# Queries projected straight into turned form in the cross attentions of layers 2 and 3 of a four-layer decoder

## The chip, the cores and the metric

One core of one Trainium2 chip runs the whole decoder in one launch. The metric is the device time of one execution in microseconds (us). The kernel before has a median of 3866.13 us over 3 runs (3862.26 to 3866.85).

## The reference, cut to what matters

The decoder has four layers, each an attention over the image context and a feed-forward part, both gated and added to x. The change touches the attentions of layers 2 and 3. For x as 4096 rows (64 batches of 64 tokens) of 256 numbers, with 16 heads of 16, they compute

```python
y = layernorm(x)
q = rms_norm(y @ Wq + bq) * gq
k = rms_norm(ctx @ Wk + bk) * gk
v = ctx @ Wv + bv
s = einsum('bqhd,bkhd->bhqk', q, k) / sqrt(16)
o = einsum('bhqk,bkhd->bqhd', softmax(s), v)
x = x + tanh(gate) * (o @ Wo + bo)
```

where `rms_norm(q)` divides a row of 256 by `sqrt(mean(q*q) + 1e-6)`. Each batch attends to its own 64 context rows. The root is one number per query row, and gq one number per column of q, so both can stand elsewhere in the product of q and k.

## The kernel before

The rows lie as 32 tiles of 128 rows (two batches) in `core.xs`. The phases of the decoder follow one another; the two that the change touches are `phase_cross` (called as `cr2` and `cr3`, once for each layer) and `KeysValues`, which makes the keys and values of both layers much earlier, beside `phase_scatter` of layer 0.

`phase_cross` is a software pipeline over the 32 tiles, written out by hand: each engine has a loop over the step s, and handles in it different tiles that lie up to seven steps apart. The engines meet at semaphores alone, and each engine works strictly in its written order. One step of the tensor engine (L1700 to L1716) has eight parts: `scores(s+1)`, `turn_y(s+4)`, `turn_probs(s)`, `project(s+3)`, `values(s-1)`, `turn_q(s+2)`, `turn_out(s-2)`, `project_out(s-3)`. A tile passes through them like this:

- VectorE takes mean and variance (L1773, L1785), GpSimd the root of the variance (L1588, L1590), VectorE writes y (L1809); PE turns y (L1614), ScalarE copies it out of PSUM (L1726).
- `project` (L1627) multiplies the turned y by Wq: 128 rows of queries by 256 columns, in PSUM. VectorE adds the bias (L1803).
- ScalarE squares the queries with a running sum per row (L1743, two instructions), GpSimd makes the root (L1594, L1596), VectorE multiplies the queries by root and by gq (`normalise`, L1765), PE turns them (`turn_q`, L1637), ScalarE copies them out of PSUM as `qT` (L1750).
- `scores` (L1650) multiplies qT by the keys, which lie in DRAM as blocks (`kbd`) and are loaded a tile at a time. VectorE takes the largest of each row and head (L1791) and subtracts it (L1795), ScalarE takes the exponential with the fixed scale 1/4 (L1737), PE turns the result (L1663), ScalarE copies it (L1733, twice a tile), `values` (L1677) multiplies it by the values, VectorE divides by the sum (L1814, L1818), PE turns (L1687), ScalarE copies (L1756), `project_out` (L1697) multiplies by Wo, and VectorE adds the gated result to x (L1778). GpSimd has added the gated bias to x before (L1602).

A product of f32 operands shows as two PE passes, each with a weight load of its own; a turn of an f32 tile of 128 by 128 as one.

`scores` waits for the copy of `qT` of its own tile, which ScalarE makes behind the exponential and the square of other tiles in the same step. `normalise` waits for the root, which waits for the square, which waits for the exponential.

`KeysValues` loads two weights, two biases and the key gain of each layer on SyncE's queue (`sync_start`), ten loads in all; PE's first product waits for all ten. Behind them on the same queue stand the context tiles and the expert weights of layer 0. It multiplies the keys by root and gain (`norm`, L1464) with the gain in `self.gain`.

## Time and profile before

| | |
|---|---|
| median of 3 runs | 3866.13 us |
| the profiled execution: time | 3858.92 us |
| its span | 3857.2 us |
| mean granted clock of TensorE | 0.865 |
| busy PE, VectorE, ScalarE, GpSimd | 2872.7, 2279.2, 1494.0, 882.5 us |
| layer 2 attention, first to last VectorE instruction | 2175.3 to 2380.9 us |
| layer 3 attention, the same | 2796.9 to 3002.4 us |

Times in rows are us from the start of the span. An engine's busy time is the time in which it has an instruction under way; matmuls overlap, so the start times of the next part say more than busy time. The two attentions take some 411 us of the span together.

### The profile page before, as it was taken

The page shows a single profiled execution, that of the slowest core. Times are in us where ns is not written, and L with a number is a line of the kernel's source. Part 1 is how long each engine was busy: PE and PEld are TensorE (multiplying, and loading weights), DVE is VectorE, ACT ScalarE, POOL GpSimd, SP SyncE. Part 2 cuts the span into 40 slices and gives each one's busy share as a digit, 9 for nine tenths or more (in the row PEclk, how much of TensorE's full clock was granted, in tenths as well). Part 3 has the DMA queues.
Part 4 walks back from the last instruction along what each step waited for, and adds up shares of the span by engine and source line. Part 5 has one row for each costly group of instructions (what it writes and reads, how often), then busy time and mean ns, then how long its engine had stood idle before and what let it go on. Part 6 is the DMA issues. An engine that isn't in the chain of part 4 may idle for free. (4 is left out here: it accounts for less than half of the span.)

```text
span 3857.2 us, 60679 instructions
## 1 busy us (share of the span) xinstructions
PE 2872.7 (74%) x19894; PEld 1814.9 (47%) x19894; DVE 2279.2 (59%) x5157; ACT 1494.0 (39%) x3085; POOL 882.5 (23%) x1238
## 2 busy tenths in 40 slices
PE   5388884365999983499536698999889509999993
PEld 4133334122555552233213476544467507888783
DVE  7699975475777766433478697888688520000003
ACT  5277771253222226399424354222255101111110
POOL 3111110475233337111100132000033061111110
PEclk7599995798999995599758799999999559999997
DMA  7766630899222225577000251000043031211214
GB/s 256 175 114 122 121 77 0 299 369 349 73 80 82 78 64 202 103 131 113 23 2 0 88 165 60 1 1 1 18 143 119 0 123 42 63 58 50 77 32 131
DMA packets 261307, 386.18 MB, mean 100 GB/s; under 512 B 56321, under 2 KB 188654, under 8 KB 260768
## 3 DMA queue, kind: packets, MB, share of 16 engines
q1 hardware_dynamic: 234192, 312.76, 30.3%
q0 software_dynamic: 25152, 68.22, 5.1%
q8 instruction: 159, 2.61, 0.3%
q10 hardware_dynamic: 1680, 1.57, 0.2%
q14 instruction: 124, 1.02, 0.1%
HBM read 227.75 MB, written 160.24 MB: 101 GB/s over the span
## 5 line engine op out<-in xcount | busy, mean ns | idle before, releaser
L2771 POOL DMA_INDIRECT rows_out<-e_out,e_tr_dest x224 | 234.6, 1047 | 874.3 <-DVE e_out L3394 523.0
L1183 ACT ACTIVATE a_pt<-a_psS 128x512 f32<-128x512 f32 x512 | 277.6, 594 | 151.9 <-PE a_psS L1081 147.5
L3394 DVE COPY e_out<-e_psD 128x512 f32<-128x512 f32 x40 | 27.7, 692 | 492.8 <-PE e_psD L3362 492.6
L1205 DVE TENSOR_REDUCE a_mx_sb<-a_psM 128x4 f32<-128x1024 f32 x256 | 293.0, 1216 | 17.3 <-PE a_psM L1064 16.1
L3162 PE MATMUL e_psG<-e_wgu,e_yT 128*128 x576 | 275.6, 601 | 27.0 <-ACT e_yT L3190 24.4
L1095 PE MATMUL a_psV<-a_pt,a_vt 128*18 128x256 f32 x4096 | 291.1, 386 | 2.1 <-issue 1.7
L3362 PE MATMUL e_psD<-e_w,e_hT 128*128 128x256 f32 x1280 | 290.2, 386 | 0.0
L3351 PE MATMUL e_psH<-e_yT,e_w 128*128 128x256 f32 x1280 | 285.2, 381 | 1.6 <-issue 0.8
L3294 ACT ACTIVATE e_hT<-e_psH 128x512 f32<-128x512 f32 x160 | 95.5, 597 | 453.1 <-PE e_psH L3351 453.1
L3362 PEld LDWEIGHTS e_psD<-e_w,e_hT 128*128 128x128 f32 x1280 | 245.8, 195 | 33.3
L3351 PEld LDWEIGHTS e_psH<-e_yT,e_w 128*128 128x128 f32 x1280 | 244.6, 191 | 35.7 <-issue 2.1
L1190 ACT ACTIVATE a_pt<-a_psS 128x1024 f32<-128x1024 f32 x256 | 241.7, 1043 | 12.6 <-PE a_psS L1081 12.4
L1081 PE MATMUL a_psS<-a_qa,a_ka 50*128 50x256 bf16 (+1 forms) x2048 | 193.1, 278 | 59.9 <-DMA a_ka<-n_pieces 36.4
L2707 POOL DMA_INDIRECT rows_in<-sc_y,sc_i x192 | 191.4, 997 | 68.2 <-issue 57.1
L3196 ACT ACTIVATE e_th<-e_gcap 128x256 f32<-128x256 f32 x144 | 60.0, 417 | 333.7 <-DVE e_ucl L3230 333.7
L1404 PE MATMUL kv_psK<-e_bgu,e_bd 128*128 128x512 f32 x256 | 127.7, 647 | 57.3 <-DMA e_bd<-ctxT 57.3
L3227 DVE TENSOR_TENSOR e_gub<-e_psG,e_bgu 128x512 f32<-128x512 f32 x144 | 99.4, 690 | 109.5 <-PE e_psG L3162 103.4
L1064 PE MATMUL a_psM<-a_ka,a_qa 48*128 48x256 bf16 x1024 | 105.9, 288 | 73.9 <-DVE a_res L1220 30.9
L1081 PEld LDWEIGHTS a_psS<-a_qa,a_ka 50*128 50x128 bf16 (+1 forms) x2048 | 74.1, 95 | 177.6 <-issue 81.1
L3179 PE MATMUL e_psO<-e_wd,e_hT 128*128 x576 | 149.3, 382 | 2.4 <-ACT e_hT L3202 1.6
L3162 PEld LDWEIGHTS e_psG<-e_wgu,e_yT 128*128 128x128 f32 x576 | 99.2, 192 | 101.4 <-issue 101.3
L1095 PEld LDWEIGHTS a_psV<-a_pt,a_vt 128*18 128x18 f32 x4096 | 86.4, 97 | 109.9 <-issue 67.8
(384 smaller groups left out, 5938.3 us busy)
## 6 DMA issues: line engine op xcount, KB each, us to landing
kbd<-e_bgu SPq DMA_DIRECT2D x64, 512.0 KB, 4.0
cr_kbd<-kbd SPq DMA_DIRECT2D x64, 512.0 KB, 3.3
rows_in<-zeros POOLq DMA_DIRECT2D x36, 522.0 KB, 6.6
e_xin<-rows_in SPq DMA_DIRECT2D x144, 128.0 KB
vbd<-e_bd SPq DMA_DIRECT2D x64, 272.0 KB, 4.2
cr_vbd<-vbd SPq DMA_DIRECT2D x64, 272.0 KB, 2.7
cq_rows<-rows_out SPq DMA_DIRECT2D x32, 512.0 KB, 5.8
e_w<-in_L_ffn_w_dram SPq DMA_DIRECT2D x16, 1024.0 KB, 7.6
```

What stands on the lines that cost most here:

```text
L1081: ins = pe.matmul(psS[:, (first + b) % S_BANKS, k * DIM:(k + 1) * DIM], at_tile(ka, rows(b, KR), t, h, slice(k * P, (k + 1) * P)), at_tile ...
L1095: ins = pe.matmul(psV[32 * q:32 * q + 2 * V, b, :], vt[:, t % 4, 2 * k + b, g, q, :], pt[:, probs(t, 4 * g + q), b, k, :], start=(g == 0 a ...
L1183: act.activation(pt[:, probs(t, h), b, :, :], psS[:, unit(t, h, b) % S_BANKS, :].rearrange("p (k c) -> p k c", k=KC), ACT.Exp, scale=scale ...
L1190: act.activation(pt[:, probs(t, h), :, :, :], psS[:, first:first + 2, :].rearrange("p b (k c) -> p b k c", k=KC), ACT.Exp, scale=scale).th ...
L1205: dve.tensor_reduce(mx[:, t % 2, :, h, :], psM[:, k % 2, :, :].rearrange("p b (f c) -> p b f c", f=2), AX_X, ALU.max).then_inc(ring_read, 1)
L1404: ins = pe.matmul(self.psK[:, u, :], self.ct[:, i % 4, k, :], self.w[:, layer, k, :], start=(k == 0), stop=(k == KC - 1))
L2707: pool.indirect_dma_start(out=rows_in[:, :], out_offset=bass.IndirectOffsetOnAxis(ap=index[u][:, k:k + 1], axis=0), in_=y[:, u, :], in_off ...
L2771: pool.indirect_dma_start(out=self.rows_out[0:limit, :], out_offset=bass.IndirectOffsetOnAxis(ap=self.dest[:, t:t + 1], axis=0), in_=rows, ...
L3162: ins = pe.matmul(psG[:, u, :], yT[:, u, k, :], wgu[:, e, k, :], start=(k == 0), stop=(k == KC - 1))
L3179: ins = pe.matmul(psO[:, u, 0:D], hT[:, u, k, :], wd[:, e, k, :], start=(k == 0), stop=(k == KC - 1))
L3351: ins = pe.matmul(psH[:, b, (f % 2) * R:(f % 2 + 1) * R], w1s[:, m, k, f * P:(f + 1) * P], yT[:, u, :, k, :], start=(k == 0), stop=(k == K ...
L3362: ins = pe.matmul(psD[:, u, tt * D:(tt + 1) * D], hT[:, u, f, tt * P:(tt + 1) * P], w2s[:, m, f, :], start=(f == 0), stop=(f == FC - 1))
```

## The change

It makes the queries directly in turned form and lets the root act later.

- `project` swaps its operands: Wq becomes the stationary side, the turned y the moving one, so the product has the 256 query columns on partitions (two blocks of 128) and the rows along it. It is made of four products of 128 columns instead of two of 256.
- VectorE adds the bias, now one number per partition, and writes `qT` itself, in three buffers instead of two. `normalise`, `turn_q` and the copy L1750 are gone.
- ScalarE squares `qT` (without a running sum); PE adds over partitions with a column of ones (`sum_squares`, in the place of `turn_q`); ScalarE copies the 128 sums out of PSUM; GpSimd makes the root with 1/16 in it, one step later than before.
- `scores` waits for the bias addition instead of the copy. The exponential takes the root as its scale, one number per row, and waits for it.
- gq is multiplied into the key gain, once: `KeysValues` loads gq of both layers (two more loads on SyncE's queue, twelve to wait for) and VectorE multiplies 128x512 once before the loop.
- The start of `phase_cross` still has five loads before its first wait: bq comes as two loads of 128 numbers, one to a partition, and the broadcast loads of bq and gq fall away.

```diff
@@ -1323,6 +1323,8 @@
+        self.query_gain = flat[:, 3584:4096].rearrange("p (l o) -> p l o", l=2)
+        self.gained = core.sem(n + "_gn")
@@ -1342,11 +1344,12 @@
     def sync_start(self, sp):
-        for layer, (wk, wv, bk, bv, gk) in enumerate(self.weights):
+        for layer, (wk, wv, bk, bv, gk, gq) in enumerate(self.weights):
+            sp.dma_start(self.query_gain[:, layer, :], gq.rearrange("(a n) -> a n", a=1).broadcast_to([P, DIM])).then_inc(self.w_loaded, 16)
@@ -1413,7 +1416,7 @@
             ins.then_inc(self.turned, 1)
-        pe.wait_ge(self.w_loaded, 16 * 10)
+        pe.wait_ge(self.w_loaded, 16 * 12)
@@ -1446,8 +1449,10 @@
             ins.then_inc(self.values_laid, 1)
     def vector_setup(self, dve):
-        dve.wait_ge(self.w_loaded, 16 * 10)
+        dve.wait_ge(self.w_loaded, 16 * 12)
+        dve.tensor_tensor(self.gain, self.gain, self.query_gain, ALU.mult).then_inc(self.gained, 1)
+        dve.wait_ge(self.gained, 1)
     def bias(self, dve, i):
@@ -1511,8 +1516,8 @@
-    q_done, q_ready, q_squared, q_based, q_rooted, q_normed, q_turned, q_copied = (
-        core.sem(n + k) for k in ("qd", "qr", "qs", "qb", "qo", "qn", "qt", "qc"))
+    q_done, q_ready, q_squared, q_summed, sum_copied, q_based, q_rooted, ones_made = (
+        core.sem(n + k) for k in ("qd", "qr", "qs", "qu", "uc", "qb", "qo", "om"))
@@ -1523,7 +1528,9 @@
-        gains = sb(ctx, n + "gains", [P, 3, DIM], F32)
+        bias_out = sb(ctx, n + "bo", [P, DIM], F32)
+        bias_q = sb(ctx, n + "bq", [P, KC], F32)
+        ones = sb(ctx, n + "ones", [P, 1], F32)
@@ -1533,10 +1540,8 @@
-        q = sb(ctx, n + "q", [P, 2, DIM], F32)
-        junk = sb(ctx, n + "junk", [P, DIM], F32)
-        qn = sb(ctx, n + "qn", [P, 2, DIM], F32)
-        qT = sb(ctx, n + "qT", [P, 2, KC, P], F32)
+        sqT = sb(ctx, n + "sqT", [P, 2, KC, P], F32)
+        qT = sb(ctx, n + "qT", [P, 3, KC, P], F32)
@@ -1558,8 +1563,9 @@
             def _(sp):
-                for m, v in enumerate((bq, gq, bo)):
-                    sp.dma_start(gains[:, m, :], v.rearrange("(a n) -> a n", a=1).broadcast_to([P, DIM])).then_inc(w_loaded, 16)
+                for k in range(KC):
+                    sp.dma_start(bias_q[:, k:k + 1], bq[k * P:(k + 1) * P].rearrange("(p a) -> p a", a=1)).then_inc(w_loaded, 16)
+                sp.dma_start(bias_out[:, :], bo.rearrange("(a n) -> a n", a=1).broadcast_to([P, DIM])).then_inc(w_loaded, 16)
                 def load_values(t):
@@ -1581,6 +1587,7 @@
             def _(pool):
+                pool.memset(ones[:, :], 1.0).then_inc(ones_made, 1)
@@ -1588,10 +1595,10 @@
-                    t = s + 3
+                    t = s + 2
-                        pool.wait_ge(q_squared, t + 1)
-                        pool.tensor_scalar(base[:, t:t + 1], square[:, t:t + 1], 1.0 / DIM, 1e-6, ALU.mult, ALU.add).then_inc(q_based, 1)
+                        pool.wait_ge(sum_copied, t + 1)
+                        pool.tensor_scalar(base[:, t:t + 1], square[:, t:t + 1], CW / DIM, CW * 1e-6, ALU.mult, ALU.add).then_inc(q_based, 1)
@@ -1609,7 +1616,7 @@
-                        pe.wait_ge(q_copied, t - 2)
+                        pe.wait_ge(sum_copied, t - 2)
                     ins.then_inc(y_turned, 1)
@@ -1623,23 +1630,26 @@
-                    for k in range(KC):
-                        ins = pe.matmul(psQ[:, 0, :], yT[:, u, k, :], wqs[:, k, :], start=(k == 0), stop=(k == KC - 1))
+                    for c in range(KC):
+                        for k in range(KC):
+                            ins = pe.matmul(psQ[:, 0, c * P:(c + 1) * P], wqs[:, k, c * P:(c + 1) * P], yT[:, u, k, :], start=(k == 0), stop=(k == KC - 1))
                     ins.then_inc(q_done, 1)
-                def turn_q(t):
+                def sum_squares(t):
-                    pe.wait_ge(q_normed, t + 1)
+                    if t == 0:
+                        pe.wait_ge(ones_made, 1)
+                    pe.wait_ge(q_squared, t + 1)
-                        pe.wait_ge(q_copied, t)
+                        pe.wait_ge(sum_copied, t)
-                        ins = pe.transpose(psT[:, 1, k * P:(k + 1) * P], qn[:, u, k * P:(k + 1) * P], core.ident[:, :])
-                    ins.then_inc(q_turned, 1)
+                        ins = pe.matmul(psT[:, 1, 0:1], sqT[:, u, k, :], ones[:, :], start=(k == 0), stop=(k == KC - 1))
+                    ins.then_inc(q_summed, 1)
                 def scores(t):
-                    u, m = t % 2, t % NK
-                    pe.wait_ge(q_copied, t + 1)
+                    u, m = t % 3, t % NK
+                    pe.wait_ge(q_ready, t + 1)
@@ -1709,7 +1719,7 @@
-                        turn_q(s + 2)
+                        sum_squares(s + 2)
@@ -1734,20 +1744,18 @@
-                        act.activation(prob[:, t % 2, :, :], prob[:, t % 2, :, :], ACT.Exp, scale=CW ** -0.5).then_inc(exped, 1)
+                        act.wait_ge(q_rooted, t + 1)
+                        act.activation(prob[:, t % 2, :, :], prob[:, t % 2, :, :], ACT.Exp, scale=rms[:, t:t + 1]).then_inc(exped, 1)
-                        if t:
-                            act.wait_ge(q_squared, t)
-                        act.activation(junk[:, :], q[:, t % 2, :], ACT.Square, accum_out=square[:, t:t + 1]).then_inc(q_squared, 1)
+                        if t >= 2:
+                            act.wait_ge(q_summed, t - 1)
+                        act.activation(sqT[:, t % 2, :, :], qT[:, t % 3, :, :], ACT.Square).then_inc(q_squared, 1)
-                        act.wait_ge(q_turned, t + 1)
-                        if t >= 2:
-                            for r in range(2):
-                                act.wait_ge(s_done[r], t - 1)
-                        act.activation(qT[:, t % 2, :, :], psT[:, 1, :].rearrange("p (k c) -> p k c", k=KC), ACT.Copy).then_inc(q_copied, 1)
+                        act.wait_ge(q_summed, t + 1)
+                        act.activation(square[:, t:t + 1], psT[:, 1, 0:1], ACT.Copy).then_inc(sum_copied, 1)
@@ -1757,16 +1765,8 @@
             def _(dve):
-                def normalise(t):
-                    u = t % 2
-                    dve.wait_ge(q_rooted, t + 1)
-                    if t >= 2:
-                        dve.wait_ge(q_turned, t - 1)
-                    dve.scalar_tensor_tensor(out=qn[:, u, :], in0=q[:, u, :], scalar=rms[:, t:t + 1], in1=gains[:, 1, :],
-                                             op0=ALU.mult, op1=ALU.mult).then_inc(q_normed, 1)
-                dve.tensor_scalar(gains[:, 2, :], gains[:, 2, :], gate, None, ALU.mult).then_inc(bias_scaled, 1)
+                dve.tensor_scalar(bias_out[:, :], bias_out[:, :], gate, None, ALU.mult).then_inc(bias_scaled, 1)
@@ -1777,8 +1777,6 @@
-                    if ok(s + 2):
-                        normalise(s + 2)
@@ -1797,10 +1795,12 @@
-                        if t >= 2:
-                            dve.wait_ge(q_squared, t - 1)
-                            dve.wait_ge(q_normed, t - 1)
-                        dve.tensor_tensor(q[:, t % 2, :], psQ[:, 0, :], gains[:, 0, :], ALU.add).then_inc(q_ready, 1)
+                        if t >= 3:
+                            for r in range(2):
+                                dve.wait_ge(s_done[r], t - 2)
+                            dve.wait_ge(q_squared, t - 2)
+                        dve.tensor_tensor(qT[:, t % 3, :, :], psQ[:, 0, :].rearrange("p (k c) -> p k c", k=KC),
+                                          bias_q[:, :].rearrange("p (k a) -> p k a", a=1).broadcast_to([P, KC, P]), ALU.add).then_inc(q_ready, 1)
@@ -3407,8 +3407,8 @@
-    key_weights = (tuple(a["L2_xattn_" + k] for k in ("Wk_img", "Wv_img", "bk_img", "bv_img", "gk_img")),
-                   (turned[1], turned[2], *(a["L3_xattn_" + k] for k in ("b_k_img", "b_v_img", "g_k_img"))))
+    key_weights = (tuple(a["L2_xattn_" + k] for k in ("Wk_img", "Wv_img", "bk_img", "bv_img", "gk_img", "gq")),
+                   (turned[1], turned[2], *(a["L3_xattn_" + k] for k in ("b_k_img", "b_v_img", "g_k_img", "g_q"))))
```

What stands on PE in one step of layer 2 before (cr_yT is the turned y, cr_wq the weight Wq, cr_psT and cr_psQ places in PSUM; here a product's two passes count as one):

```order
L1650 MATMUL cr_psS<-cr_kbd,cr_qT 64x256 x8
L1614 MATMUL cr_psT<-ident,cr_y 128x128 x2
L1663 MATMUL cr_psP<-ident,cr_prob 128x128 x8
L1627 MATMUL cr_psQ<-cr_wq,cr_yT 128x256 x2
L1677 MATMUL cr_psO<-cr_vbd,cr_pT 64x34 x16
L1637 MATMUL cr_psT<-ident,cr_qn 128x128 x2
L1687 MATMUL cr_psU<-ident,cr_o 128x128 x2
L1697 MATMUL cr_psQ<-cr_wo,cr_oT 128x256 x2
```

And now:

```order
L1660 MATMUL cr_psS<-cr_kbd,cr_qT 64x256 x8
L1621 MATMUL cr_psT<-ident,cr_y 128x128 x2
L1673 MATMUL cr_psP<-ident,cr_prob 128x128 x8
L1635 MATMUL cr_psQ<-cr_yT,cr_wq 128x128 x4
L1687 MATMUL cr_psO<-cr_vbd,cr_pT 64x34 x16
L1647 MATMUL cr_psT<-cr_ones,cr_sqT 128x1 x2
L1697 MATMUL cr_psU<-ident,cr_o 128x128 x2
L1707 MATMUL cr_psQ<-cr_wo,cr_oT 128x256 x2
```

The order of the eight parts is the same; the fourth has four products of half the width, and the sixth has two products of one column in place of two turns.

On VectorE, one step before, and one now:

```order
L1778 SCALAR_TENSOR_TENSOR xs<-cr_psQ,gates,xs 128x256
L1765 SCALAR_TENSOR_TENSOR cr_qn<-cr_q,cr_rms,cr_gains 128x256
L1785 BN_AGGR mv<-cr_st 128x2
L1791 TENSOR_REDUCE cr_mx_sb<-cr_psS 128x16
L1795 TENSOR_TENSOR cr_prob<-cr_psS,cr_mx_sb 128x1024
L1803 TENSOR_TENSOR cr_q<-cr_psQ,cr_gains 128x256
```

```order
L1778 SCALAR_TENSOR_TENSOR xs<-cr_psQ,gates,xs 128x256
L1783 BN_AGGR mv<-cr_st 128x2
L1789 TENSOR_REDUCE cr_mx_sb<-cr_psS 128x16
L1793 TENSOR_TENSOR cr_prob<-cr_psS,cr_mx_sb 128x1024
L1802 TENSOR_TENSOR cr_qT<-cr_psQ,cr_bq 128x256
```

The instruction between the addition to x and the reduction of the scores is gone; the others of the step stay in their order (beside those shown: L1809, L1814, L1818, L1773).

## Rows read from the trace of the kernel before

**Rows 1.** The page's busy time of each engine, share of the span, instructions.

```profile
PE 2872.7 (74%) x19894; PEld 1814.9 (47%) x19894; DVE 2279.2 (59%) x5157; ACT 1494.0 (39%) x3085; POOL 882.5 (23%) x1238
```

**Rows 2.** Windows: stretch, length, busy PE PEld DVE ACT POOL, clock, DMA share, GB/s.

```profile
2190.00:2200.00 10.00, 7.46 (x60) 5.77 (x61) 6.52 (x12) 5.55 (x13) 3.56 (x9) 0.83 0.33 105
2240.00:2280.00 40.00, 39.12 (x486) 29.69 (x485) 37.14 (x70) 24.22 (x56) 15.01 (x35) 1.00 0.46 143
```

**Rows 3.** Timeline, one step of layer 2, PE: start, length, instruction, [idle before <-releaser].

```profile
2261.77 1.09 PE L1650 MATMUL cr_psS<-cr_kbd,cr_qT 64*64 64x256 f32 x16
2262.79 0.44 PE L1614 MATMUL cr_psT<-ident,cr_y 128*128 128x128 f32 x2
2263.07 1.04 PE L1663 MATMUL cr_psP<-ident,cr_prob 128*128 128x128 f32 x8
2263.94 1.03 PE L1627 MATMUL cr_psQ<-cr_wq,cr_yT 128*128 128x256 f32 x4
2264.90 1.13 PE L1677 MATMUL cr_psO<-cr_vbd,cr_pT 128*64 128x34 f32 x32
2265.96 0.44 PE L1637 MATMUL cr_psT<-ident,cr_qn 128*128 128x128 f32 x2
2266.23 0.38 PE L1687 MATMUL cr_psU<-ident,cr_o 128*128 128x128 f32 x2
2266.45 1.03 PE L1697 MATMUL cr_psQ<-cr_wo,cr_oT 128*128 128x256 f32 x4
2267.61 0.64 PEld L1650 LDWEIGHTS cr_psS<-cr_kbd,cr_qT 64*64 64x64 f32 x16 [0.53 <-ACT cr_qT L1750]
```

**Rows 4.** Timeline, the same step, VectorE from `normalise` to the subtraction.

```profile
2262.39 0.94 DVE L1765 SCALAR_TENSOR_TENSOR cr_qn<-cr_q,cr_rms,cr_gains 128x256 f32<-128x256 f32 x1 [0.22 <-POOL cr_rms L1596]
2263.35 1.19 DVE L1791 TENSOR_REDUCE cr_mx_sb<-cr_psS 128x16 f32<-128x1024 f32 x1
2264.57 1.22 DVE L1795 TENSOR_TENSOR cr_prob<-cr_psS,cr_mx_sb 128x1024 f32<-128x1024 f32 x1
```

**Rows 5.** Timeline, weight loads of short products in layer 2's feed-forward part.

```profile
2444.41 0.19 PEld L2296 LDWEIGHTS bs_psC<-bs_mix,bs_scT 128*128 128x128 f32 x1 [0.24 <-issue]
2444.52 0.30 PEld L2303 LDWEIGHTS bs_psU<-bs_wu,bs_yT 128*128 128x128 f32 x2
...
2450.35 0.52 PEld L2257 LDWEIGHTS bs_psC<-bs_wr,bs_yT 128*128 128x128 f32 x4 [1.24 <-issue]
2450.79 0.30 PEld L2265 LDWEIGHTS bs_psG<-bs_wg,bs_yT 128*128 128x128 f32 x2
```

**Rows 6.** Waits, 2180 to 2590: total us, times, longest.

```profile
PEld cr_psS L1650 <- ACT cr_qT L1750: 23.5, 32, 3.2
```

**Rows 7.** Timeline, the pipeline of layer 2 filling: the first three tiles' scores.

```profile
2184.34 0.63 PE L1637 MATMUL cr_psT<-ident,cr_qn 128*128 128x128 f32 x2
...
2185.87 0.64 PEld L1650 LDWEIGHTS cr_psS<-cr_kbd,cr_qT 64*64 64x64 f32 x16 [1.30 <-ACT cr_qT L1750]
...
2191.43 0.64 PEld L1650 LDWEIGHTS cr_psS<-cr_kbd,cr_qT 64*64 64x64 f32 x16 [3.25 <-ACT cr_qT L1750]
...
2197.58 0.64 PEld L1650 LDWEIGHTS cr_psS<-cr_kbd,cr_qT 64*64 64x64 f32 x16 [1.35 <-ACT cr_qT L1750]
```

**Rows 8.** Timeline, the last steps of layer 2.

```profile
2355.09 0.64 PEld L1650 LDWEIGHTS cr_psS<-cr_kbd,cr_qT 64*64 64x64 f32 x16 [0.45 <-ACT cr_qT L1750]
...
2360.86 0.64 PEld L1650 LDWEIGHTS cr_psS<-cr_kbd,cr_qT 64*64 64x64 f32 x16 [0.68 <-ACT cr_qT L1750]
...
2364.45 1.03 PE L1697 MATMUL cr_psQ<-cr_wo,cr_oT 128*128 128x256 f32 x4
...
2366.23 0.64 PEld L1650 LDWEIGHTS cr_psS<-cr_kbd,cr_qT 64*64 64x64 f32 x16 [1.15 <-ACT cr_qT L1750]
```

**Rows 9.** The stage of the keys: a load on SyncE's queue, and a window (columns as in rows 2).

```profile
690.82 0.43 SPq L1349 DMA_DIRECT2D e_bgu<-in_L_xattn_g_k_img_dram  x1
...
740.00:780.00 40.00, 28.41 (x74) 12.08 (x73) 30.91 (x73) 20.45 (x72) 28.89 (x35) 0.94 0.97 353
```

More of the change, by code:

```diff
@@ L1498, in vector_end, with phase_cross @@
             self.lay(dve, i)
-def phase_cross(core, name, kbd_dram, vbd_dram, wq, bq, gq, wo, bo, gate, prefetch=None):
+def phase_cross(core, name, kbd_dram, vbd_dram, wq, bq, wo, bo, gate, prefetch=None):
     nc = core.nc
@@ L1601, in _ @@
                         pool.wait_ge(y_ready, t + 1)
-                        pool.tensor_tensor(core.xs[:, t, :], core.xs[:, t, :], gains[:, 2, :], ALU.add).then_inc(bias_added, 1)
+                        pool.tensor_tensor(core.xs[:, t, :], core.xs[:, t, :], bias_out[:, :], ALU.add).then_inc(bias_added, 1)
             @block.tensor
@@ L3475, in flamingo_decoder @@
         core.clear_semaphores()
-        phase_cross(core, "cr3", kbd[1], vbd[1], turned[0], a["L3_xattn_b_q"], a["L3_xattn_g_q"], turned[3], a["L3_xattn_b_o"], x_gate(3))
+        phase_cross(core, "cr3", kbd[1], vbd[1], turned[0], a["L3_xattn_b_q"], turned[3], a["L3_xattn_b_o"], x_gate(3))
         core.clear_semaphores()
```

2 lines of the change are left out of this document (1 added, 1 removed).

## The prediction, made before the changed kernel ran

> **What bounds the kernel now.** I read the page's shares first: PE is the busiest engine over the whole span [rows 1], but with 74% it does not bound every stage. So I went to windows in the two attentions. In the middle of layer 2's, PE is busy for 39.12 of 40 us and VectorE for 37.14, at full clock [rows 2]. Two engines near their end at once: only the timeline of one step tells which of them waits. The reader should see there that a step takes 5.84 us (scores of one tile at 2261.77, of the next at 2267.61) and that both engines are held up a little. PE's weight loads stand idle for 0.53 us before the scores, until ScalarE has copied qT [rows 3]; that wait comes with every tile, 23.5 us for the 32 of a layer [rows 6]. VectorE is idle for 0.22 us before `normalise`, until the root is there [rows 4]; its other nine instructions follow each other closely. The loop that sets the step runs through VectorE: subtraction, exponential, square, root, `normalise`, reduction, subtraction.
>
> **How much of PE's wait is real.** A change of tile shape costs PE something in any case. `project` (four passes of 256 columns) begins at 2263.94, and `values`, which nothing holds up, at 2264.90: 0.96 us. `project_out` has the same four passes and begins at 2266.45, so the scores could begin at 2267.41 and do so at 2267.61 [rows 3]. PE's own work in a step is thus 5.64 us, and 0.20 us is waiting. VectorE's own is 5.84 - 0.22 = 5.62. The two are nearly equal, and this decides the case: what leaves VectorE gives nothing below what PE then needs.
>
> **The change on VectorE.** `normalise` goes, 0.94 us [rows 4], and the wait before it: 5.84 - 0.22 - 0.94 = 4.68 us a step. The bias addition keeps its size (256 numbers a partition from PSUM, the added operand repeated as in the subtraction, whose 1024 numbers take 1.22 us beside the reduction's 1.19 [rows 4], so repetition costs nothing to speak of). VectorE no longer bounds.
>
> **The change on PE, step by step.**
> - `project`: eight passes of 128 columns instead of four of 256. Four such passes of the router have their weight loads from 2450.35 on, and the next product's load stands at 2450.79: 0.11 us a pass [rows 5]. The turns of the probabilities give 0.87 us for eight (2263.07 to 2263.94) [rows 3]. Eight passes take 0.87 to 0.90 us, four long ones 0.86; I take +0.03 us.
> - `sum_squares`: two products of one column, four passes, in place of two turns. No product of one column is in this trace. The nearest has 8 columns: its weight load at 2444.41 is followed by the next at 2444.52 [rows 5], so a pass takes 0.11 us although it has hardly any columns. Four passes 0.44 us, two turns 0.22 (2266.23 to 2266.45 [rows 3]): +0.22 us. From below: passes that hide wholly beside their neighbours leave only what the turns took, -0.22; from above 0.19 us a pass, the length of one load [rows 5], makes it +0.54. I take the spacing, since a load's length overlaps the pass ahead.
> - The wait before the scores goes: -0.20 us. `qT` is written by VectorE nearly two steps ahead.
>
> New PE step: 5.64 + 0.03 + 0.22 = 5.89 us, **0.05 more than now**. In the full steps the change gains nothing; the work moves to the engine that has none to spare.
>
> In the Trainium skill, TensorE: Matmul & The Clock Gate, Back-to-back issue gap, products of 1 to 64 columns follow at some 60 cycles, 25 ns. By that `sum_squares` would cost 0.1 us, the step would be 5.55 and the whole gain about 27 us, not 11. The Trainium skill has on the same page, in LDWEIGHTS (loading the stationary operand), a load of 128 columns take 128/1.2 = 107 ns; this trace's 0.11 us at 8 columns [rows 5] sides with the load.
>
> **What else waits.** After the scores are started, the chain scores 1.09, reduction 1.19, subtraction 1.22 and three hand-overs of 0.05 ends 3.7 us later, so the next scores never wait for `shifted` in a step of 5.89. `sum_squares` waits for ScalarE's square of a step before. ScalarE loses the accumulator read and the copy of 256 numbers and is busy for 24.22 of 40 us now [rows 2]; the exponential's root is made a step ahead. The prices of scale-by-row and of the 128x1 copy are not in the trace; from nothing to 0.2 us each, they lie under ScalarE's idle 40%. The new waits stand there too: behind the exponential's wait for the root on ScalarE are the square and the copy of the sums, and none of the three is late while the root is a step old. Should a VectorE instruction last longer in its new company, it has 1.2 us of new slack.
>
> **Filling.** Here the change does gain. In the first steps PE has few parts, and the loop through the root sets the pace: scores of tiles 0, 1 and 2 begin at 2185.87, 2191.43 and 2197.58 [rows 7], then every 5.84. Now:
> - tile 0: its scores wait for nothing behind `sum_squares(0)`, which begins where `turn_q(0)` did, at 2184.34, and takes four passes at the lower of the two clocks, twice 0.11 us each: it ends at 2185.2, the scores begin at 2185.3. Gain 0.6.
> - tile 0 to 1 and 1 to 2: bound by the chain of 3.7 us (PE's parts are 1.0 to 3.5). Gains 5.56 - 3.7 = 1.9 and 6.15 - 3.7 = 2.4.
> - tile 2 to 3: PE's parts without both output parts, 1.02 + 0.28 + 0.87 + 0.99 + 1.06 + 0.55 = 4.8. Gain 1.0. Tile 3 to 4: with `turn_out` 5.0. Gain 0.8.
>
> Together 6.7 us a layer. The granted clock averaged 0.83 in 2190 to 2200 [rows 2], so part of it was at 1.2 GHz, behind a wait of PE's loads of 3.25 us [rows 7]. The waits become shorter; if 3 us at 1.2 GHz stay and now fall on PE's own work, they take 1.5 us back.
>
> **Emptying.** The last step ahead of the final scores has neither `turn_y` nor `project`. In it PE could start those scores at 2364.45 + 0.96 + 0.22 = 2365.6 instead of 2366.23 [rows 8]: gain 0.6. The step before it, without `turn_y`, takes 5.77 (2355.09 to 2360.86 [rows 8]) and would take 5.89 - 0.28 + 0.06 = 5.67, if the change of shape costs a little more without the turn: gain 0.1. Behind the last scores nothing changes but the exponential's scale. Two steps ahead of these have a full load on PE and already less on VectorE, 5.77 too; there PE's 5.89 costs 0.12 each. Net gain 0.4.
>
> **Start of the phase.** Five loads stand ahead of the first wait, as before; two broadcasts of 128 KB are replaced by 256 pieces of 4 bytes. Nothing, +-0.5 us.
>
> **The keys' stage.** Two more loads on SyncE's queue, one every 0.47 us or so (the last of ten is issued at 690.82 [rows 9]): the context tiles and the expert weights behind them start 0.95 us later. The stage then is bound by transfers (DMA share 0.97 [rows 9]), so this stays: +0.95. The one VectorE product (128x512, like a bias addition) is done while PE makes its first products: 0.
>
> **The sum.** A layer: -6.7 (filling) + 23 x 0.05 = 1.15 (tiles 4 to 27) - 0.4 (emptying) = -5.95. Two layers -11.9, the keys' stage +0.95: **-11 us**. From the profiled execution's 3858.92 that is 3848; the median of the runs is 7.2 us higher than that execution, 3866.13, so I predict **3855** for the median.
>
> The Trainium skill, ScalarE: Activation LUTs, What ACT_TABLE_LOAD costs, adds about 93 ns to an ACTIVATE for a scale of one number per row. In the filling it would stand in the chain of some three exponentials a layer: the sum would be half a us less of a gain. No row here shows it.
>
> **The rivals.**
> 1. *The gain stays in the filling but half of it is lost* (clock low for a stretch, PE step 5.95 instead of 5.89). For it: PE's step was worked out from start times read to 0.01 us and from one change of shape of 0.96. Filling -13.4, clock +3, 46 x 0.11 = +5, emptying -0.8, keys +1: about -5, so 3861. Within 0.2%.
> 2. *PE's passes cost less than the load's spacing* (few columns are cheap after all, or the scores' change of shape costs less than the one before `values`). Between 5.45 (sums wholly hidden) and 5.89 I put the step at 5.6: 46 x 0.29 = 13 us more, 3842. Against it: spacings of 0.11 at 8 and at 128 columns alike [rows 5].
> 3. *Slower: PE's step grows by the loads' full length.* If the twelve short passes take 0.19 us each, the length of one load [rows 5], `project` is 1.52 and `sum_squares` 0.76 us: +0.65 and +0.32 a step. 46 x 0.97 = 45 us against the gain of 11: 3900. It decides from 6.3 us a step on, where 46 steps x 0.4 eat the gain and 8 us more. Against it: four such passes in a row took 0.44 [rows 5].
> 4. *The change does not free the scores*: they wait in the same place for the subtraction of the tile before. That chain is 3.7 us, so it would need 2 us of delays; it falls under rival 1.
>
> **How the numbers follow.** A measurement of this kernel tells about 0.2%, 7.7 us, from no change. The forecast has 0.56, rival 1 (with 4) 0.28, rival 2 0.07, rival 3 0.05, other losses of the slower kind 0.04. Most of the forecast's own width (3850 to 3859) is on the faster side of 3858.4; 0.04 of it and rival 1 are the middle. So faster 0.59, same 0.32, slower 0.09. The range takes in the forecast, rival 1 and the near part of rival 2: 3847 to 3866.
>
> **What would show it.** In the changed profile the step in the middle of layer 2 should be 5.85 to 5.93 us, with no wait on PE and VectorE idle for about 1.2 us; windows of 40 us should show VectorE at some 32 us. The scores should have no waits after tile 2, the weight loads of `sum_squares` should be 0.11 us apart, and the first two spacings of the scores 3.7 us. Each attention should be 6 us shorter, the keys' stage 1 us longer. A step under 5.75 or over 6.0 makes the prediction wrong, and so does a filling that gains less than 4 us.

## The result and the profile after

| | before | changed |
|---|---|---|
| median of 14 runs each, same chip | 3864.03 us | 3854.73 us (3843.57 to 3863.82) |
| ratio, 95% interval | 1 | 0.9978 (0.9967 to 0.9988) |
| profiled execution | 3858.92 us | 3857.75 us |
| mean granted clock of the profiled execution | 0.865 | 0.860 |

The ratio stands for 8.5 us less (4.6 to 12.7); the prediction had 11 less and a median of 3855. That the median was met to 0.3 us is partly luck: the kernel before came out 2.1 us lower than in its first three runs.

The two profiled executions differ by 1.2 us only. Stages that the change doesn't touch took longer in the second: the attention of layer 0, the same code, 451.6 and 456.6 us, and the inputs' part of layer 1's feed-forward 167.4 and 169.6. So the gain has to be read inside the two attentions, not from the spans.

The page's busy time of each engine in the changed kernel, beside [rows 1]:

```profile
PE 2897.1 (75%) x20278; PEld 1855.6 (48%) x20278; DVE 2231.4 (58%) x5094; ACT 1479.5 (38%) x3021; POOL 882.2 (23%) x1240
```

VectorE lost 48 us and PE took on 24 us. Windows over the two attentions alone, from the first load's issue to the last addition, have VectorE at 348.3 us before and 300.1 now, PE at 376.7 and 388.1: all of VectorE's loss belongs to the change, and 11 us of PE's 24. That is the change in one line: work moved to the engine that bounds. One steady step, and 100 us of such steps, as windows (columns as in [rows 2]):

```profile
2264.82:2270.71 5.89, 5.89 (x77) 4.84 (x76) 4.63 (x9) 3.25 (x7) 2.21 (x6) 1.00 0.49 147
2240.00:2340.00 100.00, 100.00 (x1292) 82.06 (x1291) 78.54 (x153) 55.08 (x120) 37.71 (x85) 1.00 0.47 138
```

PE is busy for the whole of it, VectorE for 79% where it had 93% [rows 2]. The same step on PE, as [rows 3] was before (timeline; start, length, instruction):

```profile
2264.82 1.09 PE L1660 MATMUL cr_psS<-cr_kbd,cr_qT 64*64 64x256 f32 x16
...
2265.85 0.44 PE L1621 MATMUL cr_psT<-ident,cr_y 128*128 128x128 f32 x2
...
2266.12 1.04 PE L1673 MATMUL cr_psP<-ident,cr_prob 128*128 128x128 f32 x8
...
2266.99 1.06 PE L1635 MATMUL cr_psQ<-cr_yT,cr_wq 128*128 128x128 f32 x8
...
2267.98 1.13 PE L1687 MATMUL cr_psO<-cr_vbd,cr_pT 128*64 128x34 f32 x32
...
2269.04 0.61 PE L1647 MATMUL cr_psT<-cr_ones,cr_sqT 128*128 128x1 f32 x4
...
2269.51 0.42 PE L1697 MATMUL cr_psU<-ident,cr_o 128*128 128x128 f32 x2
...
2269.76 1.03 PE L1707 MATMUL cr_psQ<-cr_wo,cr_oT 128*128 128x256 f32 x4
...
2270.72 0.45 PE L1660 MATMUL cr_psS<-cr_kbd,cr_qT 64*64 64x256 f32 x4
```

The last row is cut by the window. From scores to scores it is 5.90 us here, 5.89 or 5.90 in every full step of both layers, where it had been 5.83 or 5.84 (5.90 once a layer). The scores follow 0.96 us behind `project_out`, and the wait for qT [rows 6] is gone. The wait has changed sides. From the waits of 2220 to 2340 us in the changed kernel (total us, times, longest):

```profile
DVE xs L1778 <- PE cr_psQ L1707: 12.4, 20, 0.6
DVE cr_mx_sb L1789 <- PE cr_psS L1660: 12.1, 21, 0.6
```

VectorE now waits for PE twice in a step, 0.62 and 0.57 us.

**Where the microseconds are.** Each attention is cut at start times of the timeline: issue of wq's load, first statistics, scores of tiles 0, 4 and 31, end of the last addition to `xs`.

| part, us | layer 2 before, changed | layer 3 before, changed | forecast a layer |
|---|---|---|---|
| first issue to first statistics | 7.83, 8.54 | 9.41, 6.75 | 0 +- 0.5 |
| to scores of tile 0 | 10.33, 9.57 | 10.29, 9.53 | -0.6 |
| scores 0 to 4 (filling) | 23.37, 18.59 | 23.37, 19.47 | -6.1 |
| scores 4 to 31 | 156.99, 157.85 | 157.02, 157.85 | +0.75 |
| behind scores 31 | 14.63, 14.71 | 14.62, 14.71 | 0 |
| sum | 213.15, 209.27 | 214.71, 208.31 | -5.95 |

Measured together: -3.9 and -6.4, 10.3 us, against a forecast of 11.9. The sum is near; two of its terms are not, and they err in opposite directions.

The filling of layer 2 in the changed kernel, PE (timeline, as [rows 7]):

```profile
2187.45 1.92 PE L1635 MATMUL cr_psQ<-cr_yT,cr_wq 128*128 128x128 f32 x8
...
2190.68 1.91 PE L1635 MATMUL cr_psQ<-cr_yT,cr_wq 128*128 128x128 f32 x8
...
2192.39 0.85 PE L1647 MATMUL cr_psT<-cr_ones,cr_sqT 128*128 128x1 f32 x4
...
2193.17 1.64 PE L1660 MATMUL cr_psS<-cr_kbd,cr_qT 64*64 64x256 f32 x16
...
2197.61 1.09 PE L1660 MATMUL cr_psS<-cr_kbd,cr_qT 64*64 64x256 f32 x16 [1.20 <-DVE cr_prob L1793]
...
2199.16 0.41 PE L1621 MATMUL cr_psT<-ident,cr_y 128*128 128x128 f32 x2 [0.45 <-ACT cr_sqs L1758]
...
2201.60 1.09 PE L1660 MATMUL cr_psS<-cr_kbd,cr_qT 64*64 64x256 f32 x16
...
2203.03 0.41 PE L1621 MATMUL cr_psT<-ident,cr_y 128*128 128x128 f32 x2 [0.34 <-ACT cr_sqs L1758]
...
2206.73 1.09 PE L1660 MATMUL cr_psS<-cr_kbd,cr_qT 64*64 64x256 f32 x16
```

The spacings are 4.4, 4.0, 5.1 where the prediction had 3.7, 3.7, 4.8. Two things show here.

The first is a wait that the prediction did not have. `turn_y` may not start before ScalarE has copied an earlier tile's sums out of PSUM (L1758); both are written to `cr_psT`. ScalarE makes that copy behind the exponential and the square of other tiles. PE waits for it 0.45 and 0.34 us, between the scores of tiles 1 and 2 and of tiles 2 and 3.

The second is the granted clock. `project` takes 1.92 us ahead of the first scores and 1.06 in the steady step. The windows over the filling, scores of tile 0 to scores of tile 4: layer 2 before, then layers 2 and 3 changed (columns as in [rows 2]):

```profile
2185.87:2209.24 23.37, 17.06 (x186) 12.66 (x186) 18.01 (x32) 11.85 (x27) 7.50 (x18) 0.93 0.40 130
```

```profile
2193.17:2211.76 18.59, 16.60 (x211) 13.70 (x210) 16.06 (x30) 11.09 (x23) 7.49 (x18) 0.97 0.49 160
2809.77:2829.23 19.46, 18.69 (x211) 15.24 (x210) 16.05 (x30) 11.08 (x23) 7.50 (x18) 0.85 0.46 153
```

Between the first load and the first scores of layer 2 the mean was 0.51 before and 0.50 now, nearly all at the lower level, 1.2 GHz. In the filling proper it was 0.93 before in both layers. So in these traces the filling of layer 2 had no lower clock than before; that of layer 3 had.

### The profile page after: what moved, and what is told of

It reads as the page before. It is cut to its first block and busy times, and to the rows that moved or that the text cites. A ratio compares the mean times of both kernels' runs of the same rounds, so it can differ in the third digit from the quotient of the medians.

```text
span 3856.0 us, 61321 instructions
## 1 busy us (share of the span) xinstructions
PE 2897.1 (75%) x20278; PEld 1855.6 (48%) x20278; DVE 2231.4 (58%) x5094; ACT 1479.5 (38%) x3021; POOL 882.2 (23%) x1240
## 5 line engine op out<-in xcount | busy, mean ns | idle before, releaser
L1205 DVE TENSOR_REDUCE a_mx_sb<-a_psM 128x4 f32<-128x1024 f32 x256 | 293.0, 1214 | 19.3 <-PE a_psM L1064 18.1
```

The costliest lines, as they stand in the source:

```text
L1205: dve.tensor_reduce(mx[:, t % 2, :, h, :], psM[:, k % 2, :, :].rearrange("p b (f c) -> p b f c", f=2), AX_X, ALU.max).then_inc(ring_read, 1)
```

## The experiments

My theory after the result: PE's own work sets the steady step of the changed kernel, to a hundredth of what the rows of before gave; the filling falls short because of the clock. Rivals: a chain through VectorE still has a say in the step; the short passes cost by their number and not by what they load; the keys' stage costs more than its two issues. Each run is compared with runs of the kernel before on its own chip; where a kernel varies the changed kernel, its ratio is set against 0.9978 and its stages against the table above.

**How much of PE's wait before was slack.** An edit of the kernel before, in `turn_q`:

```diff
-                    for k in range(KC):
+                    for k in (0, 1, 0, 1):
                         ins = pe.transpose(psT[:, 1, k * P:(k + 1) * P], qn[:, u, k * P:(k + 1) * P], core.ident[:, :])
```

> The kernel before, with the two turns of the normalised queries issued twice in each step (the second pair writes the same numbers over the first): TensorE's own work in a step of phase_cross grows by 2 products of two passes each, 4 x 0.11 = 0.44 us by the spacing of such short passes. Theory of the prediction: TensorE had 5.64 us of work in the 5.84 us step of before and waited 0.20 us of it, so that the step grows by what is over 0.20: to about 5.84 + 0.24 = 6.08 us if that wait is slack, and 64 steps cost about +15 us. Rival: the step of before was set by VectorE (5.62 us of work and 0.22 us of waits) with TensorE's passes cheaper than their spacing (0.06 instead of 0.11 us): step 5.88, about +3 us. Second rival: the wait was not slack at all, the chain through the turn is what closes the step: 6.28 us, +28 us.

Measured: 3862.61 against 3862.34 us, ratio 1.0001 (0.9992 to 1.0011). The added turns are one pass each, so the expectation's own price of them was double what it had to be: in this trace the loads of four turns take 0.42 us together, 0.22 more than two.

```profile
2263.54 0.42 PEld L1637 LDWEIGHTS cr_psT<-ident,cr_qn 128*128 128x128 f32 x4
```

The steady step is 5.86 us. PE's 5.64 from the prediction and 0.22 make 5.86; 0.20 of the 0.22 went into the wait. So the wait was slack, and the working that separated PE's work from its wait holds. PE's weight loads say the same: they stand idle for 0.33 us ahead of the scores here, where they had 0.53 [rows 3], and 0.33 is also what they have in the changed kernel, which waits for nothing there. The step was not the 5.88 of the rival with 0.06 us a pass: two such passes would have left it at 5.84.

**PE as the bound of the changed kernel.** In `sum_squares`:

```diff
-                    for k in range(KC):
+                    for k in (0, 1, 0, 1):
                         ins = pe.matmul(psT[:, 1, 0:1], sqT[:, u, k, :], ones[:, :], start=(k == 0), stop=(k == KC - 1))
```

> The changed kernel, with the products that sum the squares issued twice (the second pair starts the sum again and gives the same numbers). Theory: in the changed kernel TensorE bounds the step of phase_cross (5.89 us between one scores and the next) with no slack, so that 4 more short passes of 0.11 us make 6.33 us of it, 0.44 x 62 steps = 27 us, and less the 1 to 2 steps at each end, +24 to +28 us against the changed kernel. Rival: the products stand beside other waits of TensorE's (for the exponentials' turned copy, for the squares), and the step stays within 0.1 us: +0 to +6 us.

Measured: 3881.94 us, ratio 1.0049 (1.0035 to 1.0064), 27 us over the changed kernel. Every full step is 6.34 us. Timeline, two scores:

```profile
2262.50 1.09 PE L1660 MATMUL cr_psS<-cr_kbd,cr_qT 64*64 64x256 f32 x16
...
2268.84 1.09 PE L1660 MATMUL cr_psS<-cr_kbd,cr_qT 64*64 64x256 f32 x16
```

0.44 us of passes give 0.44 us of step: no slack is left on PE.

**VectorE as the bound.** Two instructions are put on VectorE ahead of its wait for the scores:

```diff
+                    if ok(s + 2):
+                        dve.wait_ge(spared, 2 * (s + 2))
+                        for j in range(2):
+                            dve.tensor_scalar(spare[:, j, :], core.xs[:, s + 2, :], 2.0, None, ALU.mult).then_inc(spared, 1)
```

> The changed kernel, with two more VectorE instructions of 128x256 in each step of phase_cross, some 0.35 to 0.40 us each, just ahead of the wait for the scores; nothing reads what they write. Theory: VectorE went from 5.62 to 4.7 us of its own in a step, and waits for TensorE about 1.2 us of the 5.89; 0.75 us more of work is hidden, step 5.89 to 5.92 us, at most +2 us in all. Rival: VectorE is still in the chain that sets the step (projection, bias, squares, sums, and back), and the step grows by 0.3 to 0.75 us: +19 to +47 us.

Measured: 3852.27 us, ratio 0.9964 (0.9954 to 0.9975), so not slower than the changed kernel; the step is 5.89 or 5.90.

```profile
2264.15 0.48 DVE L1780 SCALAR_TENSOR_TENSOR xs<-cr_psQ,gates,xs 128x256 f32<-128x256 f32 x1 [0.40 <-PE cr_psQ L1709]
2264.55 1.02 DVE L1785 TENSOR_SCALAR cr_spare<-xs 128x256 f32<-128x256 f32 x2
...
2265.58 1.18 DVE L1795 TENSOR_REDUCE cr_mx_sb<-cr_psS 128x16 f32<-128x1024 f32 x1
```

A whole microsecond of VectorE work hides in the two waits of 0.62 and 0.57 us, of which 0.40 is left. What the change took off VectorE was worth nothing in the steady step.

**What a short pass costs.** Squares and ones in BF16, one pass a product instead of two:

```diff
-        ones = sb(ctx, n + "ones", [P, 1], F32)
+        ones = sb(ctx, n + "ones", [P, 1], BF16)
-        sqT = sb(ctx, n + "sqT", [P, 2, KC, P], F32)
+        sqT = sb(ctx, n + "sqT", [P, 2, KC, P], BF16)
```

> The changed kernel, with the squares and the column of ones in BF16, which makes one pass of each of the two summing products instead of two. Theory: TensorE bounds the step, and 2 passes of 0.11 us go from it: 5.89 to 5.67 us, 62 x 0.22 = 13.6 us faster than the changed kernel, if VectorE (4.7 us of its own) and ScalarE keep up. Rival: the chain from the projection through squares and sums closes the step, or the change of type costs ScalarE time: 5.8 us or more, less than 5 us faster. The filling should gain too, some 0.4 us a layer, since the summing passes came 0.21 us apart there. The squares are rounded to BF16, so the norms differ by up to some 0.1%.

Measured: 3822.76 us, ratio 0.9900 (0.9885 to 0.9914): 30 us faster than the changed kernel, with a step of 5.50 us. The step gained 0.40 us, not 0.22. The two attentions took 197.0 and 195.9 us by the cuts of the table, 24.7 us less together; the rest of the 30 is within the width of the two ratios. Loads and products around the sums, timeline:

```profile
2263.69 0.11 PEld L1647 LDWEIGHTS cr_psT<-cr_ones,cr_sqT 128*128 128x128 bf16 x2
...
2263.73 0.20 PEld L1697 LDWEIGHTS cr_psU<-ident,cr_o 128*128 128x128 f32 x2
...
2263.90 0.30 PEld L1707 LDWEIGHTS cr_psQ<-cr_wo,cr_oT 128*128 128x128 f32 x2
```

The next load stands 0.04 us behind the first of the two BF16 ones. In F32 (changed kernel) it stood 0.36 us behind:

```profile
2269.04 0.52 PEld L1647 LDWEIGHTS cr_psT<-cr_ones,cr_sqT 128*128 128x128 f32 x4
...
2269.40 0.29 PEld L1697 LDWEIGHTS cr_psU<-ident,cr_o 128*128 128x128 f32 x2
```

The type, then, and not only the number of passes. To tell them apart the BF16 products were issued twice, as above:

> The kernel with squares and ones in BF16 (step 5.50 us, where 5.67 had been expected), now with its two summing products issued twice. It tells what the 0.40 us were. Theory A, the type is what counts: a BF16 weight load of 128 columns follows the one before after some 0.03 us (2263.687 and 2263.702 in that trace) where an F32 one takes 0.11 us, so that two more BF16 products cost 0.03 to 0.08 us and the step is 5.53 to 5.58 us. Theory B, the number of passes is what counts (0.11 us each) and something else gave the rest of the 0.40 us: step 5.72 us. Theory C: the step of 5.50 us is already set by VectorE or a chain, and PE has slack: step 5.50 us.

Measured: 3837.41 us (two runs), ratio 0.9931 (0.9910 to 0.9953); every full step 5.55 us (timeline):

```profile
2258.04 1.09 PE L1660 MATMUL cr_psS<-cr_kbd,cr_qT 64*64 64x256 f32 x16
...
2263.59 1.09 PE L1660 MATMUL cr_psS<-cr_kbd,cr_qT 64*64 64x256 f32 x16
```

Two more BF16 products cost 0.055 us, 0.027 each; two more F32 products cost 0.44, 0.22 each, in two passes of 0.11. Theory A. It also accounts for the 0.40 us: 0.44 for the two F32 products less 0.055 for the two BF16 ones is 0.385. PE is still the bound at 5.50, since the added work shows in full. Squares and ones changed their type together, so no run tells which of the two operands counts. The time of this kernel is 12 us over that of the one with two products by the ratios, of which the step explains 2 x 27 x 0.05 = 3; its untouched attention of layer 1 took 296.0 us where the other's took 288.0, and two runs say little about the rest.

The Trainium skill, TensorE: Matmul & The Clock Gate, Weight-path perf modes — Fast Weight Load (FWL) and DoubleRow, says that a load of 128 columns is quickened when its type is not FP32, about twofold as measured. The trace agrees with the condition; by the cost of a whole pass, load and product together, the factor is 4 in this kernel (0.11 to 0.027 us). It also settles the rule that the prediction weighed, 25 ns for products of few columns: it holds here for BF16 weights (0.027 us) and not for F32 ones (0.11).

**The price of the keys' part.** Once as the changed kernel without it (edit: the loads of `gq`, the product and its wait taken out), once as the kernel before with it alone:

```diff
+            sp.dma_start(self.query_gain[:, layer, :], gq.rearrange("(a n) -> a n", a=1).broadcast_to([P, DIM])).then_inc(self.w_loaded, 16)
...
+        dve.tensor_tensor(self.gain, self.gain, self.query_gain, ALU.mult).then_inc(self.gained, 1)
```

> The changed kernel with the part that multiplies the query weights into the keys' weights taken out (the two loads, the product and the wait for it): the query weights are left out of the computation altogether. It shows that part's price. Forecast in the prediction: 0.95 us. The two traces show the time from the first instruction of the keys' stage to its first product grow from 11.3 to 14.0 us. So by the prediction this kernel is 1 us faster than the changed kernel, by the traces 2.5 to 3 us. Rival: the later start is hidden or made good in the stage after it, no difference (0 +- 0.5 us). Steps of phase_cross stay at 5.89 us in each case.

> The kernel before, with the keys' part of the change alone (query weights loaded and multiplied into the keys' weights; the queries keep theirs too, so the query weights count twice in the output). It prices that part against the kernel before. By the prediction: +0.95 us. By the start of the keys' stage in the traces (11.0 to 11.6 us to the first product without the part, 12.3 to 14.6 with it): +1 to +3 us. By the two medians of the kernel without this part and of the changed kernel, each against the kernel before (0.9960 and 0.9978): up to +7 us. The attentions of layers 2 and 3 keep their step of 5.84 us.

Measured: without it 3847.37 us, ratio 0.9960 (0.9946 to 0.9974); with it alone 3862.97, ratio 0.9999 (0.9987 to 1.0010). The first lets it cost 7 us with an interval that reaches to nothing, the second at most 4 us: by times it isn't told from nothing. The traces show the queue, first load, first context tile, first product (SyncE and PE). Before:

```profile
686.45 0.39 SPq L1347 DMA_DIRECT2D e_bgu<-in_L_xattn_Wk_img_dram  x1
...
691.29 2.36 SPq L1342 DMA_DIRECT2D e_bd<-ctxT  x4
...
697.80 8.51 PE L1404 MATMUL kv_psK<-e_bgu,e_bd 128*128 128x512 f32 x16 [30.14 <-DMA e_bd<-ctxT]
```

Changed:

```profile
690.38 0.39 SPq L1349 DMA_DIRECT2D e_bgu<-in_L_xattn_Wk_img_dram  x1
...
696.17 2.62 SPq L1344 DMA_DIRECT2D e_bd<-ctxT  x4
...
704.38 7.94 PE L1407 MATMUL kv_psK<-e_bgu,e_bd 128*128 128x512 f32 x12 [32.79 <-DMA e_bd<-ctxT]
```

The tile's load is issued 4.84 and 5.79 us behind the first: +0.95, as forecast. The product starts 11.35 and 14.00 us behind it; 11.28 without the part in the changed kernel, 12.84 with it alone in the kernel before. So 1.5 to 2.7 us at the start of the stage, more than the issues: the landing came later too. It does not show at the end of the stage: from the first of these loads to the expert layer's last product it takes 409.7 to 414.1 us in the four traces without the loads of `gq` ahead of the first product, and 408.0 to 415.1 in the eight with them. So neither the forecast's 0.95 us nor the 1.5 to 2.7 is shown to reach the time; what does stays open.

**The filling and the clock.** TensorE turns the identity while the weights land, and a little behind the first projection:

```diff
+                keep_busy(50)
                 for s in range(-4, TILES + 3):
...
                     if ok(s + 3):
                         project(s + 3)
+                        if s == -3:
+                            keep_busy(6)
```

> The changed kernel with TensorE kept at work in the filling of phase_cross: 50 turns of the identity while the weights land, 6 more behind the first projection; nothing reads what they write. In the changed kernel TensorE sits idle ahead of the filling and works it off at a low granted clock: the projections of the first two tiles take 1.92 us (1.06 in the steady steps), the first scores 1.64 and 1.98 us (1.09), the summing passes come 0.21 us apart (0.11), and the first two spacings of the scores are 4.41 and 4.02 us in layer 2, 4.88 and 4.29 in layer 3, where the prediction had 3.7 for each. Theory (the missing gain of the filling is the low clock): with the clock up, the projections take 1.06, the spacings fall to 3.7 to 3.9 us, and the filling gets 2 to 3 us a layer shorter, 4 to 6 us in all. Rival: the clock is not what sets the spacings (VectorE's and ScalarE's chain does): spacings within 0.15 us of those above, and the added work costs 0 to 2 us a layer.

Measured: 3846.17 us, ratio 0.9956 (0.9939 to 0.9973), 8 us under the changed kernel by the ratios, whose intervals overlap; by the cuts of the table the two attentions are 6.8 us shorter. Filling of layer 2, PE:

```profile
2183.43 1.06 PE L1636 MATMUL cr_psQ<-cr_yT,cr_wq 128*128 128x128 f32 x8
...
2185.59 1.06 PE L1636 MATMUL cr_psQ<-cr_yT,cr_wq 128*128 128x128 f32 x8
2186.49 0.50 PE L1648 MATMUL cr_psT<-cr_ones,cr_sqT 128*128 128x1 f32 x4
2186.92 1.09 PE L1661 MATMUL cr_psS<-cr_kbd,cr_qT 64*64 64x256 f32 x16
...
2190.81 1.09 PE L1661 MATMUL cr_psS<-cr_kbd,cr_qT 64*64 64x256 f32 x16 [1.20 <-DVE cr_prob L1801]
...
2192.81 1.91 PE L1674 MATMUL cr_psP<-ident,cr_prob 128*128 128x128 f32 x8
```

From the first statistics to the first scores it takes 6.9 us in both layers, 9.6 before this edit; the first spacing is 3.89 in both. In layer 3, with the clock up, the spacings are 3.89, 3.99, 5.19 and 5.03: 18.1 us, 1.4 less than in the changed kernel's trace. In layer 2 the clock fell again ahead of the third tile's scores (the last row: 1.91 us for eight passes, 1.04 in the steady step), which made one spacing 5.55, and the filling took 19.2 us, 0.6 more than without the edit. So the low clock cost the changed kernel 3 to 4 us a layer: 2.7 of it ahead of the first scores, where the kernel before had it as well, and behind them, set against the 18.1, 0.5 in layer 2 and 1.4 in layer 3. It explains only a part of what the filling lacks: at full clock it is still 18.1 us, not the forecast's 17.2. The waits of `turn_y` for the copy of the sums, 0.45 and 0.34 us, are there at full clock too.

**Start and best version.** For the start, VectorE's wait and the scaling of the output bias move to the step in which tile 2 is projected, and wq and bq get a semaphore of their own; the first `project_out` waits for wo:

```diff
-                    if t == 0:
-                        pe.wait_ge(w_loaded, 16 * 5)
+                    if t == 0:
+                        pe.wait_ge(q_loaded, 16 * 3)
...
-                dve.wait_ge(w_loaded, 16 * 5)
-                dve.tensor_scalar(bias_out[:, :], bias_out[:, :], gate, None, ALU.mult).then_inc(bias_scaled, 1)
+                    if s == -1:
+                        dve.wait_ge(w_loaded, 16 * 2)
+                        dve.tensor_scalar(bias_out[:, :], bias_out[:, :], gate, None, ALU.mult).then_inc(bias_scaled, 1)
```

> The changed kernel with the start of phase_cross cut loose from its loads: VectorE waits for the output bias and weights only at the fourth tile's survey, and TensorE's first projection waits for the query weights and their bias alone (a semaphore of their own). In the changed kernel's trace VectorE waits 8.27 us (layer 2) and 6.49 us (layer 3) from the first load's issue to the landing of the output weights, and the first projection starts 3.9 us behind that. Theory (the filling is a chain from the loads on): the first statistics and the first turned tile (3.1 us) run while the weights land, the projection starts about 4.5 us after the first issue instead of 12.2 and 10.4 us: 6 to 8 us a layer, 12 to 14 us faster than the changed kernel. Rival: the loads of the first keys (issued 2.3 us after the first load) land late and the first scores wait for them, which leaves 2 to 5 us a layer. Step unchanged at 5.89 us.

Measured: 3844.26 us, ratio 0.9939 (0.9918 to 0.9959), 15 us under the changed kernel. By the cuts the two attentions take 202.4 and 201.6 us: 13.6 less together. First row of statistics and first projection of layer 2; the first load was issued at 2176.74:

```profile
2176.79 0.43 DVE L1773 BATCH_NORM_STATS2 cr_st<-xs 128x6 f32<-128x256 f32 x1 [1.07 <-PEq L117]
...
2181.26 1.78 PEld L1635 LDWEIGHTS cr_psQ<-cr_yT,cr_wq 128*128 128x128 f32 x8 [0.81 <-DMA cr_bq<-in_L_xattn_bq_dram]
```

The projection starts 4.5 us behind the first issue instead of 12.2. The scores never waited for the keys' load, so the rival falls.

Then this, BF16 sums, and `gq`'s loads behind the first context tiles with the product of the gains just ahead of the first normalisation, together:

> The changed kernel with three edits together: squares and ones in BF16, the start of phase_cross cut loose from its loads, and in the keys' stage the loads of the query weights put behind those of the first context tiles, with the product of the two gains just ahead of the first key's normalisation. Sum from the runs so far: the two attentions took 208.7 and 207.8 us in the changed kernel, 12.3 us less each with BF16 squares, 6.8 less each with the early start; the keys' loads give 0 to 2 us: 38 to 40 us faster than the changed kernel, some 3815 us, 0.988 of the kernel before. Rival: with a step of 5.50 us another engine's chain shows in the filling and the two gains overlap: 30 us.

Measured: 3817.72 us, ratio 0.9885 (0.9868 to 0.9901): 36 us faster than the changed kernel and 44 faster than before. Attentions 189.6 and 188.9 us, 39.1 less together. One step as a window:

```profile
2261.49:2266.99 5.50, 5.50 (x76) 4.44 (x75) 4.63 (x9) 3.26 (x8) 2.23 (x6) 1.00 0.51 150
```

PE has 5.50 of 5.50 us: it is still the only bound. The two gains add up. The keys' first product is back at 11.57 us behind the first load.

## Why the prediction was right, point by point

- *PE's own 5.64 us and 0.20 us of wait in the step before:* right: four turns instead of two gave 5.86.
- *New step 5.89 us:* right to the hundredth, in the 50 full steps of the two layers. `project`'s eight passes, from 2266.99 to `values` at 2267.98, take 0.99 (0.96 for the four long ones), +0.03. `sum_squares` took what its F32 loads take, +0.22.
- *VectorE 4.68 us of its own:* 4.63 busy in a step, and 1 us more is hidden. The exponential's scale by row costs 0.09 us, under ScalarE's idle time; groups of ScalarE from 2220 to 2340 us, before and then changed (last numbers: busy us, mean ns, idle before):

```profile
L1737 ACT ACTIVATE cr_prob<-cr_prob 128x1024 f32<-128x1024 f32 x21 | 22.2, 1058 | 20.3 <-DVE cr_prob L1795 20.3
```

```profile
L1748 ACT ACTIVATE cr_prob<-cr_prob,cr_rms 128x1024 f32<-128x1024 f32 x21 | 24.1, 1149 | 14.2 <-DVE cr_prob L1793 14.2
```

  The Trainium skill, ScalarE: Activation LUTs, What ACT_TABLE_LOAD costs, has 93 ns for such a scale; the trace's 91 ns agrees.
- *Emptying and full steps, +0.75 a layer:* +0.86 and +0.83. The two steps with a full load gave 5.89 each, the last ones 5.68 (forecast 5.67) and 4.78.
- *Tile 0, -0.6:* -0.76 in both layers.
- *Filling, -6.1 behind tile 0:* the step that failed. It measured -4.8 and -3.9. At full clock (layer 3 of the run above) the filling is 18.1 us where the forecast left 17.2, and these 0.9 us are in three spacings. Tile 0 to 1: the chain of "3.7 us" is 3.89 (1.26 us from the scores' start to the reduction, 1.26 to the subtraction, 1.37 to the next scores; the three hand-overs were put at 0.05 each and are 0.17, 0.03 and 0.14). Tile 1 to 2: it isn't this chain that binds but PE's own parts, 3.5 us, and the wait of `turn_y` for the copy of the sums, 0.45; together 3.99. Tile 2 to 3: 5.1 to 5.2 us instead of 4.8, with 0.34 or 0.45 of the same wait. The prediction had looked at that copy and held that it is not late; in the steady steps it isn't, in the filling it is. The remainder, 0.5 us in layer 2 and 1.4 in layer 3, is PE's work at 1.2 GHz, which the prediction named and priced at up to 1.5 us, but left out of the sum.
- *Start, 0 +- 0.5:* wrong, 0.7 us longer in layer 2 and 2.7 shorter in layer 3, and it brought the sum 1.9 us nearer to the forecast. That was luck. In layer 3 the first statistics come 6.8 to 7.6 us behind the first issue in the seven traces with the changed start, 9.4 to 9.7 in the three with that of before; in layer 2 7.3 to 8.8 and 7.7 to 8.1. What ends this stretch is the landing of wo: in layer 3 it comes 4.6 us after its issue instead of 7.2, in layer 2 6.4 instead of 5.7. That two broadcasts of 128 KB less on the queue bring it forward is argued for layer 3, not shown, and why layer 2 gained nothing is open.
- *Keys, +0.95:* the queue's shift is exact; the first product is 1.5 to 2.7 us late; neither the times nor the length of the stage show what it costs in the whole.
- *Rivals:* the first (half the gain lost in the filling) came true for 1.3 and 2.2 us of the two layers' 6.1 each, with a step of 5.89 and not 5.95. The second, cheaper passes, is false for the F32 passes of the changed kernel, and came true once squares and ones were BF16. The third, 0.19 us a pass, and the fourth don't occur: in the filling PE does wait for the subtraction (1.20 us ahead of the second scores), which is the chain that the prediction counted, but in the steady steps there is no such wait.

## What to carry to other kernels

When two engines are within a few per cent of each other, taking 1 us of 5.8 from one and putting 0.25 on the other gives 0.05 the wrong way: find each engine's own work in one step first, by comparing the spacing of like instructions with and without a wait, and price the move on the engine that receives it. Small products for a sum over partitions were nearly free here in BF16 (0.027 us each) and not in F32 (0.22). And read what a phase waits for before its first instruction: the loads of an output bias and of output weights, which nothing needed for another 20 us and more, held up each of these two phases for 7 us. Together that was worth more than the whole change.

## What the runs showed of the hardware

- A product with 128x128 BF16 weights and one column cost PE 0.027 us, with F32 weights 0.22 us (two passes of 0.11), in the same place of the same loop.
- 50 turns of the identity, begun at the lower clock (layer 2: granted clock 0.50 from 2172.79 to 2176.00), took 8.45 us, between the 5.5 of all at 0.11 and the 10.6 of all at 0.21: the clock rose in their midst. In layer 2 it stayed up for the next 10 us, in which PE was busy for 7.79, and then fell; in layer 3, with the same code, it stayed. Windows of 2182 to 2196 us in that trace:

```profile
2182.00:2192.00 10.00, 7.79 (x78) 6.24 (x78) 7.63 (x20) 3.73 (x9) 4.53 (x11) 1.00 0.53 203
2192.00:2196.00 4.00, 3.64 (x20) 3.67 (x20) 2.45 (x2) 2.44 (x6) 1.53 (x4) 0.57 0.57 201
```

- A change of code that moves nothing in a stage can still find it several us longer: layer 1's attention took 288.0 to 296.0 us over the twelve traces. Medians over runs average that out; two single traces don't.
